# Who clears the block sums: a transfer from a zeroed table, or a fill by the Pool engine

## What is computed

```
xn  = layernorm(x)
msg = silu(concat(xn[src], xn[dst], edge_weight) @ mW1 + mb1)
msg = silu((layer_norm(msg) * ln_g + ln_b) @ mW2 + mb2)
agg = segment_sum(msg, src, N)                    # the block sums
gnn = xn + silu(concat(xn, agg) @ uW1 + ub1) @ uW2 + ub2
x   = x + gnn + linear_attention(xn)              # 8 heads of 64
x   = x + mixture_of_experts(layernorm(x))        # 2 of 8 experts for each node
```

## Time and profile before

| what | value |
|---|---|
| median of three runs | 1519.66 us |
| the profiled execution, its own time | 1523.24 us |
| its span, from the first to the last instruction | 1521.5 us |
| PE busy | 1325.5 us (87%) |
| DVE busy | 1170.8 us (77%) |
| ACT busy | 877.7 us (58%) |
| POOL busy | 872.7 us (57%) |
| DMA moved | 137.02 MB |
| mean granted clock of PE | 0.921 of full |

### The profile page before, as it was taken

The page is one execution under the profiler, slowest core; times in us unless marked ns, Lnnn a source line. Parts: engine busy times, 40 slices in busy tenths (PEclk is TensorE's granted clock), DMA queues, the critical chain, the costliest instruction groups (busy, mean ns, idle before and its releaser), DMA issues.

```text
span 1521.5 us, 32009 instructions
## 1 busy us (share of the span) xinstructions
PE 1325.5 (87%) x8815; PEld 1143.2 (75%) x8816; DVE 1170.8 (77%) x3538; ACT 877.7 (58%) x1697; POOL 872.7 (57%) x880
## 2 busy tenths in 40 slices
PE   4665799988299999999999999999998847999991
PEld 1455677767199999999999999999885644777771
DVE  7999767752299999999999999999972586444442
ACT  1342234432178778888788887788772443665560
POOL 2288771002188777777777777777720015666651
PEclk7656899989599999999999999999999978999996
DMA  6500120002234333333333333334880082444447
GB/s 180 119 5 4 41 62 20 1 19 67 102 104 111 99 99 106 101 100 106 99 107 101 101 108 101 99 107 94 90 203 1 1 307 46 70 66 69 69 55 267
DMA packets 71241, 137.02 MB, mean 90 GB/s; under 512 B 23082, under 2 KB 43724, under 8 KB 70551
## 3 DMA queue, kind: packets, MB, share of 16 engines
q0 software_dynamic: 36560, 77.33, 23.2%
q1 hardware_dynamic: 33842, 55.71, 11.8%
q10 hardware_dynamic: 780, 3.24, 0.5%
HBM read 110.91 MB, written 25.29 MB: 90 GB/s over the span
## 4 chain that ended last, share of the span: by engine, by line
PE 71%; DVE 16%; DMA 6%; issue 3%; ACT 3%; POOL 2%; ACTq 0%; DVEq 0%; POOLq 0%; SPq 0%
PE ps L1024 11%; PE ps L784 9%; PE ps L1122 7%; PE ps L998 6%; PE ps L997 6%; PE ps L1002 6%; PE ps L1014 6%; DVE place_val_t L1495 3%; DMA msg_t<-dst_table,stage_idx 2%; DVE lane_hot_e_t L1490 2%; DMA near_rows<-row_list 2%; PE ps L1151 2%; PE ps L1150 2%; PE ps L1152 2%; PE ps L1055 2%
## 5 line engine op out<-in xcount | busy, mean ns | idle before, releaser
L707 POOL DMA_INDIRECT msg_t<-dst_table,stage_idx x448 | 440.9, 984 | 129.0 <-issue 127.2
L997 PE MATMUL ps<-w_hi_t,msg1T_hi_t 128*128 128x256 f32 x896 | 252.7, 304 | 0.0
L1277 ACT ACTIVATE msg_t<-msg_t 128x512 f32<-128x512 f32 x224 | 141.7, 632 | 178.6 <-DVE msg_t L1688 177.5
L1265 ACT ACTIVATE msg1n_t<-msg_t,nw_b,nw_y 128x256 f32<-128x256 f32 x448 | 242.2, 590 | 0.0
L998 PE MATMUL ps<-w_lo_t,msg1T_hi_t 128*128 128x256 f32 x896 | 234.4, 283 | 0.0
L1024 PE MATMUL ps<-msg_t,hot_t 128*125 128x256 f32 x896 | 230.4, 379 | 0.0
L676 POOL DMA_INDIRECT sorted_edges<-sort_sb_t,chunk_to x112 | 139.3, 1244 | 85.8 <-DVE chunk_to L1482 52.3
L1002 PE MATMUL ps<-w_hi_t,msg1T_lo_t 128*128 128x256 f32 x896 | 179.9, 282 | 0.0
L998 PEld LDWEIGHTS ps<-w_lo_t,msg1T_hi_t 128*128 128x128 f32 x896 | 172.1, 192 | 0.0
L997 PEld LDWEIGHTS ps<-w_hi_t,msg1T_hi_t 128*128 128x128 f32 x896 | 170.6, 190 | 0.0
L694 POOL TENSOR_TENSOR nw_y<-nw_v,minus_half 128x4 f32<-128x4 f32 x112 | 116.7, 1042 | 92.5 <-DVE nw_v L1650 88.4
(11 more groups left out here) (367 smaller groups left out, 3016.5 us busy)
## 6 DMA issues: line engine op xcount, KB each, us to landing
near_rows<-row_list SPq DMA_DIRECT2D x44, 320.0 KB
w_sb_t<-in_L_ffn_W_dram SPq DMA_DIRECT2D x16, 512.0 KB, 8.5
msg_t<-dst_table,stage_idx POOLq DMA_INDIRECT x448
res_t<-in_x_dram SPq DMA_DIRECT2D x1, 3125.0 KB
total<-zero_chunks_t SPq DMA_DIRECT2D x1, 3125.0 KB
dst_table<-dst_stage SPq DMA_DIRECT2D x25, 125.0 KB
agg_t<-total SPq DMA_DIRECT2D x1, 3125.0 KB
xm_table<-xm_t POOLq DMA_DIRECT2D x5, 625.0 KB, 7.5
```

Of the source, the lines that this page charges most:

```text
L707: pool.indirect_dma_start(out=msg1[:, k, j, :], out_offset=None, in_=dst_table, in_offset=bass.IndirectOffsetOnAxis(stage_idx[:, G * k + j ...
L997: pe.matmul(o[j], part(msg1T_hi, j, c), w2_hi[:, c, :], start=(c == 0), stop=False)
L1265: m = A(msg1n[:, (kl + 1) % 2, j, :], msg1[:, kk, j, :], ACT.Identity, bias=nw_b[:, kk, j:j + 1], scale=nw_y[:, kk, j:j + 1])
L1277: A(v, v, ACT.Silu).then_inc(msg1_sb, 1)
```

## The change

The transfer `agg <- totals[1]` on SP's queue and SP's two waits in front of it go. POOL gets the same two waits and then one fill of `agg` with zeros, after its first twelve gathers and ahead of its first power. DVE, which waited for the transfer ahead of its first addition to `agg` (step 9 of the loop), now waits for the fill. The transfer that zeroes `totals[1]` in DRAM stays, and so does DVE's earlier wait for it.

```
@@ sync
             sp.wait_ge(side_out, 48)
-            sp.wait_ge(hpre_ps, len(CH))
-            sp.wait_ge(mixed_ps, NB)
-            sp.dma_start(agg[0:NP], totals[1][0:N].rearrange("(p t) d -> p t d", p=NP)).then_inc(total_zero, 16)
             sp.wait_ge(w_lo_ok, W2_LO)
@@ gpsimd
             for m in range(AHEAD_UNITS):
                 gather(m)
+            pool.wait_ge(hpre_ps, len(CH))
+            pool.wait_ge(mixed_ps, NB)
+            pool.memset(agg[:], 0.0).then_inc(fills, 1)
             pool.wait_ge(token_ok, 1)
@@ vector
                 if isinstance(m_, int) and m_ == 0:
-                    dve.wait_ge(total_zero, 32)
+                    dve.wait_ge(fills, N_FILL + 1)
```

## The result

| | before | changed |
|---|---|---|
| executions | 4 | 4 |
| median of the four | 1520.08 us | 1494.9 us |
| median without the execution of 4707.97 us | 1519.66 us | 1494.9 us |
| the profiled execution | 1523.24 us | 1494.18 us |
| ratio of the times | | 0.9837, 95% interval 0.9818 to 0.9857 |

The change makes the kernel faster by 1.6%, that is by 24.8 us (1519.66 less 1494.9). One execution of the kernel before took 4707.97 us and is left out of the ratio.

The account below looks back on a forecast made before the run. The prediction took the loop's start to be bound by the first `near_rows` transfer, stuck behind the `agg` transfer; landing it 24.9 us earlier, with the fill free, gave 1519.66 - 24.9 = 1494.8 us, range 1491.5 to 1498.5.

Parts of the forecast that it names:

- What bounded the start: Ahead of the edge loop: first `near_rows` transfer takes 28.28 us, queued behind the `agg` transfer on five of sixteen DMA engines.
- The rival that `near_rows` was slow by itself: Ahead of the loop: `near_rows` takes 28 us without `agg` too, time stays at 1519.7 us; chance 0.02.
- The landing alone: First `near_rows` transfer with nothing ahead of it: 3.5 us, bounds 2.8 and 6.8, landing 24.9 us earlier.
- The fill: POOL's new fill ahead of its first power: 6400 elements in 5.5 us, from about 375.5 to 381.0.
- the slow rows of another form: Slow-fill rival on POOL: 5.1 to 5.9 ns an element, 1516.5 to 1521.5 us; chance 0.04.
- The cover: POOL before its first power, needed at 386.4: the fill has 10.9 us, twice what it needs.
- its price is nothing: POOL's fill ends before the first power is needed, so it was to cost 0 us.
- This rival: DVE's first comparison waits for POOL's fill, starting at 381.0: 1.7 us less gain, 1496.5 us; chance 0.03.
- The clock: PE's clock at the loop's start: same half clock expected, shifted; rival, back sooner, up to 4.1 us more, chance 0.10.

Follow-up runs that it names:

- the spread transfer: Kernel before, with the clearing transfer kept ahead of `near_rows` but cut into 112 and 13 rows: 1746.96 us on chip B, ratio 0.9946 to the kernel before.
- the double fill: Changed kernel with POOL's fill of `agg` done twice in a row: 1736.86 us on chip B, ratio 0.9888 to the kernel before.
- chip D: One of three further chips for follow-up runs; the kernel before took 1752.97 us there, the changed kernel 1729.72 us.
- chip A: The chip of the main runs, kernel before against changed kernel: 1519.66 us and 1494.9 us.

## Why the prediction was right

The forecast was 1494.8 us; 1494.9 us was measured, and the main reason named, the transfer ahead of `near_rows`, is the one that the runs show. That the two agree to 0.1 us is luck: one term of 1.4 us was missing from the sum, and something else, most of it unexplained, made up for it.

- *What bounded the start:* right. With the transfer out of the way of `near_rows`, 28.28 us become 3.47 (changed kernel), and the same happens when it is kept but issued behind (3.47 us, PE's standing still 4.39 us). That five of sixteen DMA engines carried it was read from a share of 0.30, and the spread transfer's share of 1 at twice the rate bears it out. The rival that `near_rows` was slow by itself is out.
- *The landing alone:* 3.5 us forecast, 3.47 measured; on the other chips it was 3.45 to 3.50 in five traces, 3.76 and 3.98 in two, all inside the forecast's bounds of 2.8 and 6.8. The 2.75 us that the prediction works out from the Trainium skill (DMA: Bandwidth & Descriptors, "Anatomy of one DMA") are an estimate from a fit that the page gives for transfers of POOL's path, and this one is issued by SP; every trace shows more. SP issued it 0.09 us after DVE's split had ended (373.31 + 0.69 = 374.00), against 0.16 us before: 0.07 us gained by SP's shorter list, 0.09 forecast.
- *The fill:* 5.5 us forecast from two short rows, 5.44 measured in each trace with the fill in one instruction on POOL (5.46 for the second of the double fill). The slope of contiguous float32 fills held over a factor of 38 in length; the slow rows of another form said nothing about it.
- *The cover:* the first power was forecast at 386.4 and came at 386.50, with the fill's end at 379.27 instead of 381.0. POOL's first power waited for DVE and not for the fill.
- *What failed:* the term that put the fill at "its price is nothing". Its cover was worked out for POOL's queue alone. DVE's first comparison starts 1.6 us before the fill ends and was held for it, 1.76 us long instead of 0.3, so 1.4 us of the 24.9 were given back, and the start of the loop follows the fill's end and no longer the landing. This rival stood in the prediction at 0.03, with 1.7 us as its price. The evidence against it was misread: line 1645 never took over 537 ns in a loop with POOL busy 157 of 200 us. But in the double fill the hold was as long as the fill, and that loop has no fill in it: POOL's powers there are 1.05 us long and write four elements. Rows without a fill could neither show such a hold nor exclude it.
- *Why the time fits all the same:* 24.9 - 1.4 = 23.5 at the loop's start would be 1496.2 us; chip D agrees with 23.07 us at the start and 23.3 in the time, and the trace of chip A with 23.6 at the 188th comparison. The times of chip A differ by 24.8 us, 1.3 more than 23.5. The clock returned 0.6 us sooner after PE's start, and PE does twice the work in these 0.6 us, which is worth 0.3 us. The ratio's interval, 0.9818 to 0.9857, is 1492.0 to 1497.9 us on the 1519.66 of before and holds both numbers, so the remaining 1 us may be noise; no run settles it.
- *The clock:* it fell and came back as before, shifted. With PE standing still 1.60 us, the first product ran at 0.38 us a matmul instead of 0.58, that is at the upper level (2.4 GHz and not 1.2). The windows from the same run show that the clock fell about a microsecond later all the same (0.53 over 2 us is 0.1 us at the upper level):

```profile
452.00:454.00 2.00, 0.71 (x6) 0.72 (x7) 0.47 (x2) 1.63 (x3) 0.07 (x1) 1.00 0.34 122
454.00:456.00 2.00, 1.54 (x9) 1.25 (x7) 1.51 (x4) 0.63 (x1) 0.00 (x0) 0.53 0.13 47
```

Whether still less standing still would keep it up can't be told from these runs.

The Trainium skill (SBUF — State Buffer, "Who interferes with whom") states that a `tensor_scalar` can take the mode that needs the shared ports and then blocks or is blocked for a whole instruction, while a `tensor_tensor` with two SBUF inputs collides only with a POOL instruction that reads. The trace agrees with both, 5.59 us for the one beside a fill and 0.42 for the other. The runs show which form is held and for how long; that shared ports are the reason is the page's account and was not tested. By that rule the forecast would have been 1496.5 us.

## What to carry to other kernels

When one engine stands still behind a small transfer, look at what was issued just ahead of it on the same queue and on how many DMA engines that runs: a share near 0.3 over a long stretch was here the sign that the small one waited for the part of itself behind the large one. Clearing on chip what that transfer cleared gave nearly the whole wait back (24.8 of 28.5 us), and filling the region piece by piece as it fell free took the hold off the start. When a long instruction goes to POOL, price it twice, once against POOL's own next instruction and once against the `tensor_scalar` that DVE runs beside it; short instructions elsewhere in the trace don't show that collision.

## What the hardware showed that I had not expected

- A POOL fill of 128x6400 float32 held a DVE `tensor_scalar` of 125x256 for its whole rest: 1.76 us and, beside a second fill, 5.59 us instead of 0.32. The same comparison as `tensor_tensor` took 0.42 us beside the same fill.
- A 3.2 MB transfer that ran on while the gathers started delayed one of them to 11.46 us from issue to landing, while the mean share of the DMA engines was 0.45 to 0.55.
- Spread over sixteen engines, the same transfer ran at 269 to 282 GB/s, twice and not three times the rate on five.
- On three other chips the kernel before took 1753 us instead of 1520, with the same durations of every instruction looked at (the fill 5.44 us, the comparison 0.32) and 132 us of waits in the loop for what is most likely the gathered rows.
